# Eight layer norms in one kernel: two halves of 16 tiles, unrolled, with a TensorE wait for each tile

## The reference

```python
def _layernorm(x, axis=-1, eps=1e-05):
    m = jnp.mean(x, axis=axis, keepdims=True)
    v = jnp.var(x, axis=axis, keepdims=True)
    return (x - m) / jnp.sqrt(v + eps)

x = L0_attn_x
x = x + _L0_attn_ref(_layernorm(x, axis=-1), ...)   # dn: delta net
x = x + _L0_ffn_ref(_layernorm(x, axis=-1), ...)    # sf: sine ffn
x = x + _L1_attn_ref(_layernorm(x, axis=-1), ...)   # tt: test-time mlp
x = x + _L1_ffn_ref(_layernorm(x, axis=-1), ...)    # de: dense experts
x = x + _L2_attn_ref(_layernorm(x, axis=-1), ...)   # sa: attention, norms once more inside
x = x + _L2_ffn_ref(_layernorm(x, axis=-1), ...)    # cm: channel mix
x = x + _L3_attn_ref(_layernorm(x, axis=-1), ...)   # ba: blocked attention
x = x + _L3_ffn_ref(_layernorm(x, axis=-1), ...)    # rf: routed ffn
```

## Time and profile before

| what | us |
|---|---|
| median of 3 timed runs | 3606.04 (3604.13 to 3606.18) |
| the profiled execution | 3612.15 |
| its span, first to last instruction | 3610.3 |
| TensorE busy | 2505.6 (69%) |
| VectorE busy | 1809.9 (50%) |
| ScalarE busy | 1295.6 (36%) |
| GpSimd busy | 717.2 (20%) |

### The profile page before, as it was taken

One profiled execution on the slowest core, in us unless ns is written; L12 is line 12 of the kernel. 1 busy time (PEld: TensorE's weight loads), 2 busy tenths in 40 slices (PEclk: granted clock), 3 DMA queues, 4 the chain that ended last, 5 costly groups with the idle time before them and its releaser, 6 DMA issues.

```text
span 3610.3 us, 65131 instructions
## 1 busy us (share of the span) xinstructions
PE 2505.6 (69%) x20692; PEld 1381.9 (38%) x20744; DVE 1809.9 (50%) x3541; ACT 1295.6 (36%) x2627; POOL 717.2 (20%) x1299
## 2 busy tenths in 40 slices
PE   2330695767676766675499999544898998988954
PEld 1220463445455545342234444331333333333433
DVE  2115255642222222366366666354777777777353
ACT  1111010522222221101156566322666666666512
POOL 3551132024444444002001111010000000000012
PEclk8565555867777686686599999665999999999766
DMA  1122421000000000000411110005111111111000
GB/s 30 42 53 49 98 61 40 0 6 0 0 0 0 0 0 0 7 0 13 143 28 30 27 27 22 3 16 139 29 29 31 27 31 30 28 31 27 10 14 23
DMA packets 129382, 103.26 MB, mean 29 GB/s; under 512 B 52254, under 2 KB 108967, under 8 KB 129002
## 3 DMA queue, kind: packets, MB, share of 16 engines
q1 hardware_dynamic: 129258, 101.55, 10.9%
HBM read 58.96 MB, written 41.94 MB: 28 GB/s over the span
## 4 chain that ended last, share of the span: by engine, by line
PE 50%; DVE 16%; POOL 11%; issue 11%; SPq 4%; ACT 4%; DVEq 2%; DMA 1%; POOLq 0%; ACTq 0%; PEldq 0%
PE psum L1811 9%; PE psum L1823 7%; PE psum L1800 6%; PE psum L1835 5%; SPq L1737 3%; DVE ba_blockmax L2029 2%; DVE X L1195 2%; PE psum L586 1%; POOL dn_ss L745 1%; POOL dn_vscale L746 1%; PE psum L1341 1%; PE psum L1328 1%; PE psum L1359 1%; PE psum L382 1%; ACT ba_pt L1899 1%
## 5 line engine op out<-in xcount | busy, mean ns | idle before, releaser
L2029 DVE TENSOR_REDUCE ba_blockmax<-psum 128x16 f32<-128x1024 f32 x512 | 609.2, 1221 | 200.3 <-PE psum L1800 196.9
L1899 ACT ACTIVATE ba_pt<-psum 128x512 f32<-128x512 f32 x1024 | 542.1, 601 | 286.5 <-PE psum L1811 286.4
L1800 PE MATMUL psum<-ba_ks,ba_qs 64*128 64x512 bf16 x1024 | 362.8, 433 | 45.4 <-DMA ba_ks<-ba_kstk 31.1
L1811 PE MATMUL psum<-ba_qs,ba_ks 64*128 64x512 bf16 x1024 | 335.4, 403 | 82.9 <-DVEq L59 51.5
L2031 DVE TENSOR_REDUCE sa_negmax<-psum 128x1 f32<-128x1024 f32 x256 | 304.5, 1221 | 164.6 <-PE psum L1800 164.2
L1899 ACT ACTIVATE sa_pt<-psum 128x512 f32<-128x512 f32 x512 | 268.7, 602 | 201.0 <-PE psum L1811 124.2
L1823 PE MATMUL psum<-ba_pt,ba_vh 128*32 128x512 f32 x2048 | 306.1, 673 | 0.0
L1800 PE MATMUL psum<-sa_ks,sa_qs 96*128 96x512 bf16 x512 | 200.1, 396 | 52.0 <-DMA sa_ks<-sa_kstk 31.3
L1811 PEld LDWEIGHTS psum<-ba_qs,ba_ks 64*128 64x128 bf16 x1024 | 80.2, 95 | 394.9 <-issue 366.0
L1811 PE MATMUL psum<-sa_qs,sa_ks 128*128 128x512 bf16 x460 | 175.4, 385 | 22.0 <-DVEq L59 19.4
L1942 POOL CAST ba_mparts<-ba_negmax 128x8 bf16<-128x8 f32 x64 | 12.2, 191 | 821.5 <-DVE ba_negmax L2044 821.5
(11 more groups left out here) (468 smaller groups left out, 4543.8 us busy)
## 6 DMA issues: line engine op xcount, KB each, us to landing
ba_qs<-ba_qstk SPq DMA_DIRECT2D x128, 96.0 KB, 2.1
ba_ks<-ba_kstk SPq DMA_DIRECT2D x128, 96.0 KB, 2.2
sa_qstk<-sa_pq SPq DMA_DIRECT2D x48, 128.0 KB
sa_kstk<-sa_pk SPq DMA_DIRECT2D x48, 128.0 KB
sa_qs<-sa_qstk SPq DMA_DIRECT2D x32, 192.0 KB, 2.6
sa_ks<-sa_kstk SPq DMA_DIRECT2D x32, 192.0 KB, 2.7
ba_qstk<-ba_pq SPq DMA_DIRECT2D x48, 128.0 KB, 2.3
ba_kstk<-ba_pk SPq DMA_DIRECT2D x48, 128.0 KB, 2.3
```

Source lines behind the costliest of these rows:

```text
L1800: last = nc.tensor.matmul(bank(2 * slot + h), qs[b][0:KP, :].rearrange("p (a r) -> p r a", r=NTB)[:, r, :], ks[b][0:KP, h * HALF:(h + 1) * ...
L1811: nc.tensor.matmul(bank(4 + slot), ks[b][K0:P, x_ * P:(x_ + 1) * P], qs[b][K0:P, h * HALF:(h + 1) * HALF], start=True, stop=True).then_inc ...
L1899: nc.scalar.activation(pt[2 * x_ + h][:, :], bank(4 + slot), ACT.Exp, scale=SCALE).then_inc(pt_in, 1)
L2029: ins = nc.vector.tensor_reduce(blockmax[g][:, r, :], src.rearrange("p (n s) -> p n s", s=BLOCK), AXX, ALU.max, negate=True)
```

## The change

`layer_norm` alone is changed, and with it all eight norms. Statistics, aggregation, eps and power are made in two halves of 16 tiles; VectorE goes on with the second half's statistics while GpSimd takes the first half's power. All loops are written out. `ready` is raised by each normalised tile and TensorE waits for each tile. `turned` and `written` stay as they are, once for a group. For the second norm of sa the halves go through the chain one after the other.

```diff
+    halves = [slice(h * NT // 2, (h + 1) * NT // 2) for h in range(2)]
...
-        with v.Fori(0, NT // 8) as i:
-            for n in range(8):
-                c.do(nc.vector.bn_stats(stats[:, bass.ds(i * 8 + n, 1), :], k.X[:, bass.ds(i * 8 + n, 1), :]))
-            c.restart()
-        for n in range(NT):
-            c.do(nc.vector.bn_aggr(mv[:, n, :], stats[:, n, :]))
-        c.sync()
-        nc.vector.tensor_scalar(tmp[:, 0, :], mv[:, :, 1], EPS, None, ALU.add).then_inc(var_in, 1)
-        v.wait_ge(root_out, 1)
+        for at in halves:
+            for n in range(at.start, at.stop):
+                c.do(nc.vector.bn_stats(stats[:, n, :], k.X[:, n, :]))
+            c.sync()
+            for n in range(at.start, at.stop):
+                c.do(nc.vector.bn_aggr(mv[:, n, :], stats[:, n, :]))
+            c.sync()
+            nc.vector.tensor_scalar(tmp[:, 0, at], mv[:, at, 1], EPS, None, ALU.add).then_inc(var_in, 1)
         if twice:
...
+            for h, at in enumerate(halves):
+                v.wait_ge(root_out, h + 1)
+                c.step(nc.vector.tensor_tensor(tmp[:, 0, at], rstd[:, at], rstd[:, at], ALU.mult))
+                c.step(nc.vector.tensor_tensor(tmp[:, 1, at], tmp[:, 0, at], mv[:, at, 1], ALU.mult))
+                nc.vector.tensor_scalar(tmp[:, 0, at], tmp[:, 1, at], EPS, None, ALU.add).then_inc(var_in, 1)
+        for g in range(NG):
+            i, z = g // 2, g % 2
+            if g % (NG // 2) == 0:
+                h = 2 * g // NG
+                v.wait_ge(root_out, (3 if twice else 1) + h)
+                if twice:
+                    c.step(nc.vector.tensor_tensor(rstd[:, halves[h]], rstd[:, halves[h]], root[:, halves[h]], ALU.mult))
+            v.wait_ge(turned[z], i + 1)
+            for n in range(GROUP):
+                t = g * GROUP + n
+                nc.vector.tensor_scalar(xn[z][:, n, :], k.X[:, t, :], mv[:, t, 0:1], rstd[:, t:t + 1],
+                                        ALU.subtract, ALU.mult).then_inc(ready[z], 1)
         c.restart()
...
     def tensor(t):
         k.start(t, layer)
-        with t.Fori(0, NG // 2) as i:
-            for g in range(2):
-                t.wait_ge(ready[g], i + 1)
-                t.wait_ge(written[g], i + 1)
-                for n in range(GROUP):
-                    last = nc.tensor.transpose(k.psum[:, g, n * P:(n + 1) * P], xn[g][:, n, :], k.ident[:, :])
-                last.then_inc(turned[g], 1)
+        for g in range(NG):
+            i, z = g // 2, g % 2
+            t.wait_ge(written[z], i + 1)
+            for n in range(GROUP):
+                t.wait_ge(ready[z], GROUP * i + n + 1)
+                last = nc.tensor.transpose(k.psum[:, z, n * P:(n + 1) * P], xn[z][:, n, :], k.ident[:, :])
+            last.then_inc(turned[z], 1)
...
         for q in range(2 if twice else 1):
-            p.wait_ge(var_in, q + 1)
-            nc.gpsimd.tensor_tensor((root if q else rstd)[:, :], tmp[:, 0, :], k.mhalf[:, 0:NT], ALU.pow).then_inc(root_out, 1)
+            for h, at in enumerate(halves):
+                p.wait_ge(var_in, 2 * q + h + 1)
+                nc.gpsimd.tensor_tensor((root if q else rstd)[:, at], tmp[:, 0, at], k.mhalf[:, 0:NT // 2], ALU.pow).then_inc(root_out, 1)
```

More of the change, by code:

```diff
@@ L154, in vector @@
-        c.restart()
-        with v.Fori(0, NG // 2) as i:
-            for g in range(2):
-                v.wait_ge(turned[g], i + 1)
-                for n in range(GROUP):
-                    t = i * 2 * GROUP + g * GROUP + n
-                    last = nc.vector.tensor_scalar(xn[g][:, n, :], k.X[:, bass.ds(t, 1), :], mv[:, bass.ds(t, 1), 0],
-                                                   rstd[:, bass.ds(t, 1)], ALU.subtract, ALU.mult)
-                    if n < GROUP - 1:
-                        c.do(last)
-                c.sync()
-                last.then_inc(ready[g], 1)
-            c.restart()
+        for at in halves:
[6 more added lines that the diff above has]
+            nc.vector.tensor_scalar(tmp[:, 0, at], mv[:, at, 1], EPS, None, ALU.add).then_inc(var_in, 1)
@@ L168, in tensor @@
+        c.restart()
     def tensor(t):
         k.start(t, layer)
-        with t.Fori(0, NG // 2) as i:
-            for g in range(2):
-                t.wait_ge(ready[g], i + 1)
-                t.wait_ge(written[g], i + 1)
-                for n in range(GROUP):
-                    last = nc.tensor.transpose(k.psum[:, g, n * P:(n + 1) * P], xn[g][:, n, :], k.ident[:, :])
-                last.then_inc(turned[g], 1)
+        for g in range(NG):
[5 more added lines that the diff above has]
+            last.then_inc(turned[z], 1)
@@ L181, in scalar @@
             a.wait_ge(*affine_in)
-        with a.Fori(0, NG // 2) as i:
-            for g in range(2):
-                a.wait_ge(turned[g], i + 2)
-                dst = k.XT[:, bass.ds(i * 2 * GT + g * GT, GT)]
-                if place is not None:
-                    nc.scalar.copy(place(i, g), k.psum[:, g, :].rearrange("p (c t) -> p c t", t=P // B)).then_inc(written[g], 1)
-                elif affine is None:
-                    nc.scalar.copy(dst, k.psum[:, g, :]).then_inc(written[g], 1)
-                else:
-                    nc.scalar.activation(dst, k.psum[:, g, :], ACT.Identity, scale=affine[0],
-                                         bias=affine[1]).then_inc(written[g], 1)
+        for g in range(NG):
+            i, z = g // 2, g % 2
+            a.wait_ge(turned[z], i + 2)
+            dst = k.XT[:, g * GT:(g + 1) * GT]
+            if place is not None:
+                nc.scalar.copy(place(i, z), k.psum[:, z, :].rearrange("p (c t) -> p c t", t=P // B)).then_inc(written[z], 1)
+            elif affine is None:
+                nc.scalar.copy(dst, k.psum[:, z, :]).then_inc(written[z], 1)
+            else:
+                nc.scalar.activation(dst, k.psum[:, z, :], ACT.Identity, scale=affine[0], bias=affine[1]).then_inc(written[z], 1)
     def gpsimd(p):
```

5 lines of the change are left out of this document (removed).

## The result

The changed kernel takes **3495.19 us** (median of 4 runs, 3490.95 to 3499.06), the kernel before 3606.11 beside it (4 runs, 3604.13 to 3615.8): a ratio of **0.9686**, 95% interval 0.9668 to 0.9705. The direction was forecast, the size not quite: 3511 was named, and the time lies 5 us under the low end of the range, 3500. The kernel before had 3617.33, 3615.92 and 3614.0 beside the later experiments, so the gain of 110.9 between these two medians leans on a low value of the kernel before.

What follows compares the result with a forecast made beforehand. Eight norms run as exposed serial chains while other engines idle, though TensorE holds half the critical chain. Six norms gain 73.2 us; with sa and ba 95.3, so 3612.15 becomes 3516.9, less 6.1 for timed runs: 3511, range 3500 to 3537.

Steps and rivals of the forecast that it cites:

- Statistics and powers: In a norm: normalising can start 9.3 us after first statistics; powers run 4.8 to 7.7 and 9.4 to 12.3.
- Normalising: VectorE's 32 normalising operations in a norm: 1.15 us for a group of four, 9.2 for eight groups.
- The drain: End of a norm, after VectorE's last tile: one transpose, the copy's start and the copy, 1.3 us, before 1.9.
- table load: dn's norm: copies' table loaded once instead of in every pass, charged 0.4 us; dn's gain 12.8.
- sa and ba: Norms with GpSimd memsets behind the powers: gains 14.0 and 11.5 us if interleaving, 10.5 and 8.2 if VectorE is shut out.
- Straight code: Writing out all norm loops: costs between nothing and one microsecond stall in each norm, 8 us in all.
- Rival 1: In the norms, the second power blocks the first half's normalising: 24.3 us back, 3535; chance 0.22.
- Rival 2: In the norms, a wait per tile breaks TensorE's transpose pipeline: 62 us back, 3573; chance 0.05.
- Rival 3: In tt's loop, TensorE's granted clock falls from 0.75: 0.62 adds 95 us, 0.5 gives 3640; chance 0.03, 0.02 slower.

Runs made afterwards that it cites:

- the written-out before: Kernel before with only dn's 32 transposes written out, group waits kept: 3604.92 us against 3614.0, ratio 0.9979.
- the second pair of executions: Kernel before and changed kernel each run once more, unchanged, for their traces: 3618.23 us and 3488.5 us.

## Why the prediction was off

- **Statistics and powers**: right. The first normalising comes 9.0 after the first statistics (forecast 9.3; I had given 0.1 to each wait, and they cost less), the powers run from 4.8 and 9.2, and the second is done at 12.1, before the second half wants it at 13.1.
- **Normalising**: the term of the sum that failed. I took 1.15 for a group, 9.2 for eight; measured 1.04 and 8.3. "I take 1.15 for a group with its wait for `turned`" carried over the longer step at a group's head from a loop in which TensorE begins at the fourth tile. With TensorE waiting for whole groups that step is still there (9.0 from first to last start in tt, which is 1.17 a group); with the wait per tile it is gone (8.0). The change itself removed the cause of a number that I took from before.
- **The drain** of 1.3 measured 1.0: from the end of the last normalising (2225.4 + 0.35) to the last copy's start pass 0.4, where I had put 0.65 for the transpose and the copy's start. These three make 1.5 a norm, and the six norms without memsets give 81.6 instead of 73.2. dn's norm, with its table load, is 0.8 us longer than a plain one, not 0.4.
- **sa and ba**: the two cases were priced well. In sa VectorE was shut out and ended at 30.1 (31.5 forecast for that); in ba the engines interleaved, last copy 22.9 (23.3). I had taken the middle of both, and it came out as one of each: 23.8 against 22.1. Each was, as before, the kind that its own layer had shown; why the two layers differ stays open.
- **Straight code, "between nothing and one stall of a microsecond in each norm"**: the step that put the time outside the range, since the range's low end had the faster normalising in it: the 105.4 us of the norms alone give 3500.6, just inside. No stall showed inside a norm. But code that is written out also moves all that stands behind it in TensorE's stream, and dn's part behind its norm, with its stalls for issue, came out 8 us cheaper, and tt lost a stall of 3 us, which the pair of executions in the table doesn't show, tt's rest being 2.6 longer in it. The sign wasn't open in my bounds: I had only allowed for a loss. Stalls put down to issue stood in the trace of before, and I had not asked what they hang on. By the written-out before, whose dn came out 10.5 shorter, the bound should have reached from about -10 to +8.
- **Rival 1** (the second power holds up normalising, 3535) is refuted: 341 to 360 ns in cm beside it, and 4.19 us beside two powers as beside none. **Rival 2** (TensorE can't follow per tile): its transposes keep one tile behind. **Rival 3** (the clock) didn't come: the row that answers to the earlier trace rows is this.

```profile
780.00:1430.00 650.00, 460.13 (x1999) 334.87 (x1999) 159.75 (x498) 142.90 (x409) 263.50 (x449) 0.73 0.00 0
```

The granted clock is 0.73 in the same stretch where it was 0.75, TensorE is busy for 460 us where it was 455, and both are far from the 0.62 from which the rival decides. tt's work lies 32.8 us earlier now; the stretch moved by as much, 747.2 to 1397.2, has 0.73 and 460 too, and so has the second execution of the kernel before in 780 to 1430 (0.73, 459). The rival's price at a clock of 0.5 is a wrong sum: 455 x (0.75/0.5 - 1) is 227 us, so 3511 would become 3738, 132 over before, and not 3640.

**Taken together**: 1.5 a norm and the two memset cases are the 10 us in the norms, dn's part 7.7 of the 9 outside. Against the profiled execution's own time I had 3612.15 - 95.3 = 3516.9, and it took 3497.54: 10.1 from the norms, 9.0 from outside them and 0.3 from rounding and what lies around the span. The 9.0 are one draw: the second pair of executions has 24.1. And 3511 starts from a median of 3606.04 for the kernel before; from any of its later ones, 3614.0 to 3617.33, the same sum would have come out another 8 to 11 us too high.

## What to carry to other kernels

Cut a serial chain through several engines into halves when each piece's cost goes with its size, and let the consumer wait per piece; here the three parts of the change (no loops 6.6 us, halves 5.4, a wait per tile 2.0) simply added up. Before a duration is carried over from the old code, ask which wait it contains and whether the change removes it. Where an engine runs through hundreds of tiny instructions, look for stalls at a fixed spacing in its instruction stream: an edit ahead of them that adds or takes away instructions can move them, worth microseconds of either sign (dn 10.5 shorter with its transposes written out in the kernel before, 6.1 longer with them back in a loop in the changed one), and then the edit's own worth needs a control with the same instruction count on that engine.

## What the runs showed of the hardware that I had not expected

- A GpSimd power (2.9 us for 16 columns) doesn't slow VectorE's normalising at all (4.19 us for 16 beside two powers), while a GpSimd multiply of 128x1024 holds one for its whole 1.9 us and a row of ten memsets holds one up to 7.0 us.
- Putting these memsets beside statistics instead of normalising is worth 5.5 us in sa and 3.8 in ba, and this kernel is the fastest, 3481.33.
- TensorE stood still for 2 to 7 us at a time in stretches of 32x32 matmuls, waiting for nothing else that the trace shows; each of the stalls looked at ended 1.3 to 1.4 us after a packet of 16384 bytes, but for the last one after, 1.9. The one in tt, ahead of the transpose behind a jump, ended 1.4 to 1.6 after one. That it waits for instructions is inferred from this.
- Parts that no kernel here touched differ by up to 6 us between two executions of one kernel (tt's rest 713.7 and 719.8 before). ba's rest is 1025 to 1028 us in the three executions with the old norm of ba and 1016 to 1024 in the eleven with the new; nothing tried tells why.
